# Splitting the last down weights beside the gate products, the rest from tile 1 on, and half of the first LoRA matrices asked for by GpSimd

## The chip, the cores and the metric

One core of one Trainium2 chip. The metric is the device time of one execution in microseconds (us), lower is better. TensorE (PE) multiplies, VectorE (DVE), ScalarE (ACT) and GpSimd (POOL) work on elements, SyncE (SP) mostly asks for transfers; SP, ACT and POOL each have a queue of their own for those requests (SPq, ACTq, POOLq in the rows).

## What is computed

128 sequences of 32 tokens with 512 features, so 4096 tokens; two adapted layers, of which the first contains all that the change touches:

```python
def _L0_cond_ref(x, adapter_mapping, W, b, lora_As, lora_Bs):    # A, B: one rank-16 pair per sequence
    base_out = jnp.einsum('bti,oi->bto', x, W) + b
    A, Bm = lora_As[adapter_mapping], lora_Bs[adapter_mapping]
    return base_out + jnp.einsum('btr,bro->bto', jnp.einsum('bti,bir->btr', x, A), Bm) * SCALING
def _L0_ffn_ref(x, W_gate, W_up, W_down):                        # 512 -> 1376 -> 512
    h = jax.nn.silu(x @ W_gate.T) * (x @ W_up.T)
    return h @ W_down.T
x = x + _L0_ffn_ref(_L0_cond_ref(x, slots, ...), W_gate, W_up, W_down)
x = x + _L1_ffn_ref(_L1_cond_ref(x, languages, ...), ...)        # routed low-rank experts, no nonlinearity between
```

## The kernel before, in words

Every float32 operand of a product is split in two parts that TensorE takes at full rate: ScalarE writes the high part (`..._hi`), VectorE subtracts it from the original and writes the low part (`..._lo`). A product is then three: high by high, high by low, low by high (`mm3`). The tokens are cut into `NT` = 8 tiles of 512; `KC` = 4 chunks of 128 features; `NF` = 11 chunks of the 1376 hidden features, `NP` = 5 pairs of them and one single; `NS` = 4 pairs of tiles.

**The prologue** goes over the tiles t = 0 to 7 (the first adapted linear layer). For each tile TensorE runs base products for four output chunks (`cond_base`), the tile's A products after the second chunk (`lora_in`; in tile 0 before the last quarter of the base products), and at the end the B products (`cond_lora`). ScalarE copies the four closed banks out (`close_c`, line 1015), GpSimd stores them to a scratch tensor (line 942). The A matrices of a tile come as `NG` = 2 groups of `GB` = 8 sequences, one small request (32 KB, 256 B rows) per sequence, on SyncE's queue: `gather_a`, line 559. Each takes its address from a register, which `load_slots` (line 550) fills from a table that must have landed. A group of the next tile can be asked for once `a_lo` of the same group is made for this tile. ScalarE and VectorE turn them to `a_hi`, `a_lo` (`turn_a`, lines 998 and 1437). B rows come by an indirect gather on GpSimd's queue (`gather`, line 816), whose row numbers `row_i` VectorE makes from `slot_i`.

**Weights of the feed-forward part** are also split once and stored to scratch tensors in memory. They are combined first, in a scheme with seven products in place of eight: each block needs four sums, made by GpSimd (`gate_up_sums`, `down_sums`). Gate and up weights are made beside the products of the first pair of tiles, `LEAD` = 10 products ahead, in a ring `wring` of 12 slots, and are stored from there (line 574). Down weights are made in `d_steps`: three groups (two pairs of chunks, two pairs, one pair) of seven steps, and one step for the single chunk. A step is a high part (`down_hi`, line 1042, ScalarE), a low part (`down_lo`, line 1467, VectorE) and a store on SyncE's queue (`store_down`, line 624), from four buffers `dt`. `load_down` (line 612) fetches the raw weights into two buffers `wd_raw`. `d_due(t, m)` says which step stands behind closing chunk m of tile t: one for each from (0, 1) to (5, 2), 22 steps in all. All these buffers lie in the region that the operands of the gate products take later.

**The order on each engine is fixed by the program**, and every wait holds up all that stands behind it on its engine. On SyncE a tile's turn is: requests for A of the next tile and x of the tile after (`load_x`, line 545), `load_down`, `load_slots`, then the stores of this tile's `dt` steps.

**After the prologue**, for each pair of tiles: 77 gate and up products ("slots" of 6 matmuls), then 35 down products and the single ones. From slot 77 on the weights come back through `load_slot` (line 604), whose first call waits for all `dt` stores.

## Time and profile before

| | us |
|---|---|
| three runs | 990.55, 992.14, 992.19 (median 992.14) |
| the profiled execution | 990.57 |
| its span, first to last instruction | 988.8 |
| PE busy in it | 976.7 |
| DVE, ACT, POOL busy | 589.7, 464.2, 273.1 |
| mean granted clock of TensorE | 0.997 of full |

The profile is one execution. Times in rows are us from the span's start. A row of a timeline gives start, duration, engine, line and operation, what is written from what, how many were merged (x16), and in brackets the engine's idle time before it and what ended it. Consecutive matmuls overlap in it: each is shown with 0.39 us but they start 0.227 us apart at full clock. The prologue lies in the first 152 us.

### The profile page before, as it was taken

The page shows a single profiled execution, that of the slowest core. Times are in us where ns is not written, and L with a number is a line of the kernel's source. Part 1 is how long each engine was busy: PE and PEld are TensorE (multiplying, and loading weights), DVE is VectorE, ACT ScalarE, POOL GpSimd, SP SyncE. Part 2 cuts the span into 40 slices and gives each one's busy share as a digit, 9 for nine tenths or more (in the row PEclk, how much of TensorE's full clock was granted, in tenths as well). Part 3 has the DMA queues.
Part 4 walks back from the last instruction along what each step waited for, and adds up shares of the span by engine and source line. Part 5 has one row for each costly group of instructions (what it writes and reads, how often), then busy time and mean ns, then how long its engine had stood idle before and what let it go on. Part 6 is the DMA issues. An engine that isn't in the chain of part 4 may idle for free.

```text
span 988.8 us, 14263 instructions
## 1 busy us (share of the span) xinstructions
PE 976.7 (99%) x4723; PEld 825.7 (84%) x4723; DVE 589.7 (60%) x969; ACT 464.2 (47%) x854; POOL 273.1 (28%) x276
## 2 busy tenths in 40 slices
PE   8989999999999999999999999999999999999998
PEld 6878888888888888888888888888888899898986
DVE  4555587676794433496333398243268488786862
ACT  4654657655671333472333375233357274545342
POOL 3543343564400622310431330072140470000000
PEclk9989999999999999999999999999999999999999
DMA  7898886766977876777986787887679650606132
GB/s 236 268 389 285 278 280 233 269 215 252 323 267 249 296 238 193 249 231 257 314 278 194 207 288 247 276 304 199 192 256 347 236 191 22 237 23 234 64 107 86
DMA packets 131730, 230.14 MB, mean 233 GB/s; under 512 B 30789, under 2 KB 30790, under 8 KB 131146
## 3 DMA queue, kind: packets, MB, share of 16 engines
q1 hardware_dynamic: 127720, 216.63, 66.0%
q0 software_dynamic: 3936, 12.61, 3.5%
q8 instruction: 39, 0.64, 0.3%
q14 instruction: 33, 0.27, 0.1%
q10 hardware_dynamic: 2, 0.00, 0.0%
HBM read 165.74 MB, written 63.44 MB: 232 GB/s over the span
## 4 chain that ended last, share of the span: by engine, by line
PE 89%; SPq 4%; DVE 3%; issue 1%; DMA 1%; ACT 1%; DVEq 0%; ACTq 0%
PE bank L1863 89%; SPq L559 3%; DMA a_raw<-in_a_cols 1%; PE bank L2016 1%; DVE cop_lo L1484 1%; DVE a_lo L1437 1%; DVE dt L1467 0%; SPq L545 0%; SPq L550 0%; SPq L558 0%; DVE wring L1462 0%; ACT c_out L1015 0%; SPq L624 0%; DVE b_lo L1440 0%; DVE c L1493 0%
## 5 line engine op out<-in xcount | busy, mean ns | idle before, releaser
L1863 PE MATMUL bank<-cop_hi,wring 128*128 128x512 f32 x1234 | 380.4, 389 | 0.2 <-ACT c_out L1015 0.2
L1863 PEld LDWEIGHTS bank<-cop_hi,wring 128*128 128x128 f32 x1234 | 231.6, 188 | 48.5 <-ACT c_out L1015 0.4
L1863 PE MATMUL bank<-cop_lo,wring 128*128 128x512 f32 x616 | 239.6, 389 | 0.0
L1863 PE MATMUL bank<-op_hi,wring 128*128 128x512 f32 x560 | 173.7, 389 | 0.0
L1512 DVE TENSOR_TENSOR v<-bank,p7s 128x512 f32<-128x512 f32 x44 | 30.4, 691 | 202.9 <-PE bank L1863 202.9
L1863 PEld LDWEIGHTS bank<-cop_lo,wring 128*128 128x128 f32 x616 | 115.6, 188 | 24.0
L1863 PEld LDWEIGHTS bank<-op_hi,wring 128*128 128x128 f32 x560 | 105.1, 188 | 22.0 <-DMA wring<-wd_scratch 0.2
L1863 PE MATMUL bank<-op_lo,wring 128*128 128x512 f32 x280 | 108.9, 389 | 0.0
L1114 ACT ACTIVATE s<-bank 128x512 f32<-128x512 f32 x44 | 26.3, 599 | 119.0 <-PE bank L1863 118.7
L1498 DVE TENSOR_TENSOR op_lo<-h,op_hi 128x512 fp32r<-128x512 f32 x100 | 72.6, 743 | 3.7 <-ACT op_hi L1071 3.4
L861 POOL TENSOR_TENSOR h_t<-h,h 128x512 f32<-128x512 f32 x20 | 26.5, 1326 | 163.1 <-DVE h L1534 163.1
L1071 ACT ACTIVATE op_hi<-h 128x512 fp32r<-128x512 f32 x100 | 62.6, 626 | 13.3 <-PE bank L1863 12.4
L1083 ACT ACTIVATE bank<-bank 128x512 f32<-128x512 f32 x44 | 25.6, 582 | 77.1 <-PE bank L1863 77.1
L1863 PEld LDWEIGHTS bank<-op_lo,wring 128*128 128x128 f32 x280 | 52.6, 188 | 10.8
L900 POOL TENSOR_TENSOR t_sum<-x_second,x_second 128x256 f32<-128x256 f32 x12 | 8.9, 776 | 175.8 <-DMA x_second<-x_scratch 175.8
L1863 PE MATMUL bank<-xa_hi,w_hi 128*128 128x512 f32 x128 | 51.2, 400 | 1.6 <-DVE w_lo L1429 1.1
L1863 PE MATMUL bank<-xa_lo,w_hi 128*128 128x512 f32 x128 | 50.9, 398 | 0.0
L1863 PE MATMUL bank<-xa_hi,w_lo 128*128 128x512 f32 x128 | 50.7, 396 | 0.0
L1517 DVE TENSOR_TENSOR p7s<-bank,p7s 128x512 f32<-128x512 f32 x44 | 30.4, 692 | 24.8 <-PE bank L1863 24.6
L1090 ACT ACTIVATE p7s<-bank 128x512 f32<-128x512 f32 x44 | 26.3, 599 | 30.6 <-PE bank L1863 30.6
L1105 ACT ACTIVATE s<-bank 128x512 f32<-128x512 f32 x44 | 26.3, 598 | 30.6 <-PE bank L1863 30.6
L1098 ACT ACTIVATE bank<-bank 128x512 f32<-128x512 f32 x44 | 25.6, 582 | 30.0 <-PE bank L1863 30.0
(226 smaller groups left out, 1932.6 us busy)
## 6 DMA issues: line engine op xcount, KB each, us to landing
wring<-wgu_scratch SPq DMA_DIRECT2D x231, 256.0 KB, 3.0
wring<-wd_scratch SPq DMA_DIRECT2D x140, 256.0 KB, 5.5
wgu_scratch<-wring SPq DMA_DIRECT2D x77, 256.0 KB, 3.4
c_scratch<-c_out POOLq DMA_DIRECT2D x32, 256.0 KB
c<-c_scratch SPq DMA_DIRECT2D x32, 256.0 KB, 4.1
xs_raw<-x_scratch SPq DMA_DIRECT2D x16, 512.0 KB, 5.6
out<-res SPq DMA_DIRECT2D x32, 256.0 KB, 2.1
x_raw<-in_x SPq DMA_DIRECT2D x15, 512.0 KB, 6.5
```

The lines of the kernel that those rows point to most:

```text
L559: e.dma_start(a_raw[:, g, b, :], a_cols[bass.ds(slot, 1)].rearrange("s p c -> (s p) c")).then_inc(a_in[g], DMA)
L861: e.tensor_tensor(h_t3[p][:, :], h22[p][:, :], h12[p][:, :], ALU.subtract).then_inc(t3_done, 1)
L1071: e.activation(op_hi[n % N_OP][:, :], op_source[i][p][:, :], ACT.Copy).then_inc(op_hi_done, 1)
L1083: e.activation(bank_y[b][:, :], bank_a[b][:, :], ACT.Copy).then_inc(ay_done, 1)
L1090: e.activation(p7s[b][:, :], bank_w[b][:, :], ACT.Copy).then_inc(p7s_done, 1)
L1098: e.activation(bank_z[b][:, :], bank_y[b][:, :], ACT.Copy).then_inc(yz_done, 1)
L1105: e.activation(s1[j % 2][:, :], bank_a[j % 2][:, :], ACT.Silu).then_inc(silu1_done, 1)
L1114: e.activation(s2[j % 2][:, :], bank_z[j % 2][:, :], ACT.Silu).then_inc(silu2_done, 1)
L1498: e.tensor_tensor(op_lo[n % N_OP][:, :], op_source[i][p][:, :], plain(op_hi[n % N_OP][:, :]), ALU.subtract).then_inc(op_lo_done, 1)
L1512: e.tensor_tensor(v[b][:, :], bank_z[b][:, :], p7s[b][:, :], ALU.add).then_inc(gc22_done, 1)
L1517: e.tensor_tensor(p7s[b][:, :], bank_y[b][:, :], p7s[b][:, :], ALU.add).then_inc(gc21_done, 1)
L1863: return e.matmul(out_ap, lhs, rhs, start=start, stop=stop, skip_group_check=True)
```

## The change

Three things, which do not depend on each other's values:

- GpSimd asks for the second group of tile 0's A: it waits for the table, loads 8 registers and issues 8 requests ahead of its gather of B. SyncE asks for the first group alone. The load of `slot_i` goes from SyncE's queue to ScalarE's.
- The two large groups of down steps (14) stand from chunk 1 of tile 1 to chunk 0 of tile 5: three steps in tile 1, three in tile 2, four in tile 3, three in tile 4, one in tile 5 (`d_at`). `load_down(0)` and `load_down(1)` go to the ends of SyncE's turns for tiles 0 and 1.
- The last group and the single chunk, now two halves (9 steps), go beside the gate products of the first pair, one step in each block of seven from block 1 to block 9 (`d_late`), with buffers of their own. They are loaded at the start of that stage, their sums stand behind `gate_up_sums(3)` on GpSimd, and each store stands on SyncE behind a gate store. `load_c(1, 0)`, which fills one of the borrowed regions, waits for the last step; the seventh operand of the down products waits for all stores.

```diff
--- before.py
+++ after.py
...
+    within(cst_region, 5 * ROW)
+    wd_late = work("wd_late", [2, D], F32)
+    wd_single = work("wd_single", [D], F32)
+    ds_late = [work(f"ds_late{i}", [2 * P], F32) for i in range(4)]
+    dt_late = [sb(f"dt_late{i}", [2, 2 * P], F32R, op_region + n * ROW)
+               for i, n in enumerate((N_OP - 2, N_OP - 1, 2 * N_OP - 2, 2 * N_OP - 1))]
...
     a_in = [sem(f"a_in{g}") for g in range(NG)]
-    b_in = sem("b_in")
+    a_first_in, b_in = sem("a_first_in"), sem("b_in")
     c_stored = [sem(f"c_stored{m}") for m in range(KC)]
...
     dt_stored = [sem(f"dt_stored{i}") for i in range(4)]
-    ws_stored = sem("ws_stored")
     w_moved = [sem(f"w_moved{i}") for i in range(N_W)]
...
     n_groups = (NP + 1) // 2
-    d_steps = [(g, i) for g in range(n_groups) for i in W_ORDER]
+    d_steps = [(g, i) for g in range(n_groups) for i in W_ORDER] + [("s", b) for b in range(2)]
     d_turn = {st: n for n, st in enumerate(d_steps)}
+    N_D, N_EARLY = len(d_steps), len(W_ORDER) * (n_groups - 1)
+    d_at = [KC + 1 + n * (KC * (NT - 3) - 3) // N_EARLY for n in range(N_EARLY)]
...
-        n = KC * t + m - 1
-        return [n] if 0 <= n <= len(d_steps) else []
-    def dt_stores(r):
-        return len([n for n in range(len(d_steps)) if n % 4 == r])
+        return [n for n in range(N_EARLY) if d_at[n] == KC * t + m]
+    def d_late(j):
+        return [N_EARLY + j - 1] if 0 < j <= N_D - N_EARLY else []
+    def dt_stores(r, steps=N_D):
+        return len([n for n in range(steps) if n % 4 == r])
...
     def d_views(n):
-        if n == len(d_steps):
-            src = wd_raw[n_groups % 2][:, 0, 0, :].rearrange("p (b c) -> p b c", b=2)
-            return dt_[n % 4][:, :, 0, :], dt_[n % 4][:, :, 1, :], src
         g, i = d_steps[n]
+        if g == "s":
+            return dt_late[n % 4][:, 0, :], dt_late[n % 4][:, 1, :], wd_single[:, 2 * P * i:2 * P * (i + 1)]
+        if g == n_groups - 1:
+            src = {1: wd_late[:, 0, 0:2 * P], 2: wd_late[:, 1, 0:2 * P], 4: wd_late[:, 1, 2 * P:],
+                   5: ds_late[0][:, :], 6: ds_late[1][:, :], 7: ds_late[2][:, :], 3: ds_late[3][:, :]}[i]
+            return dt_late[n % 4][:, 0, :], dt_late[n % 4][:, 1, :], src
         c, r = pairs_of(g), wd_raw[g % 2]
...
                 e.wait_ge(cop_lo_done, cop_n(s, q, C_ORDER[0]) - 1)
+            if (s, q) == (1, 0):
+                e.wait_ge(dt_lo_done, N_D)
             if s > 1 and q == 0:
...
                     e.wait_ge(dt_stored[r], DMA * dt_stores(r))
-                e.wait_ge(ws_stored, DMA)
             if n == N_SLOT:
...
         def load_down(g):
-            if g >= 2:
-                e.wait_ge(dt_lo_done, d_turn[g - 2, 3] + 1)
-            if g < n_groups:
-                n = pairs_of(g)
-                src = w_down[:, 4 * g:4 * g + 2 * n, :].rearrange("p (r k) d -> p r k d", r=n)
-                e.dma_start(wd_raw[g % 2][:, 0:n, :, :], src).then_inc(wd_in[g % 2], DMA)
-            else:
-                e.dma_start(wd_raw[g % 2][:, 0, 0, :], w_down[:, 2 * NP, :]).then_inc(wd_in[g % 2], DMA)
+            n = pairs_of(g)
+            e.dma_start(wd_raw[g][:, 0:n, :, :], w_down[:, 4 * g:4 * g + 2 * n, :].rearrange(
+                "p (r k) d -> p r k d", r=n)).then_inc(wd_in[g], DMA)
+        def load_down_late():
+            e.wait_ge(cop_lo_done, 14)
+            e.dma_start(wd_late[:, :, :], w_down[:, NF - 3:NF - 1, :]).then_inc(wd_in[0], DMA)
+            e.dma_start(wd_single[:, :], w_down[:, NF - 1, :]).then_inc(wd_in[1], DMA)
...
             e.wait_ge(dt_lo_done, n + 1)
-            if n == len(d_steps):
-                e.dma_start(ws_dram,
-                            plain(dt_[n % 4][:, :, :, :]).rearrange("p b h c -> p b (h c)")).then_inc(ws_stored, DMA)
+            g, i = d_steps[n]
+            if n >= N_EARLY:
+                to = ws_dram[:, i, :] if g == "s" else wd_dram[g, i][:, 0, :]
+                e.dma_start(to, plain(dt_late[n % 4][:, :, :]).rearrange("p h c -> p (h c)")).then_inc(
+                    dt_stored[n % 4], DMA)
                 return
-            g, i = d_steps[n]
             c = pairs_of(g)
...
             e.dma_start(w0_raw[:, part, :], w0[:, part, :]).then_inc(w0_in[ks[0]], DMA)
-        e.dma_start(slot_i[:, :], slots.unsqueeze(1).to_broadcast([GB, R, n_batch // GB])).then_inc(slots_in, DMA)
         e.wait_ge(slot_list_in, DMA)
         load_slots(0)
-        gather_a(0)
+        gather_a(0, (0,))
         for ks in x_parts(1):
             load_x(1, ks)
-        load_down(0)
         load_slots(1)
...
                     load_x(t + 2, ks)
-            if t == 1:
-                load_down(1)
+            if t < 2:
+                load_down(t)
             if t + 2 < NT:
...
                     store_down(n)
-                    for g in (2, 3):
-                        if n == d_turn[g - 2, 3]:
-                            load_down(g)
+        load_down_late()
         for n in range(7, N_G):
...
                 load_gate_up(n // 7 + 2)
+            if (n - LEAD) % 7 == 6:
+                for k in d_late((n - LEAD) // 7):
+                    store_down(k)
+        for j in range((N_G - LEAD) // 7, NF):
+            for k in d_late(j):
+                store_down(k)
         for n in range(N_G, NS * N_SLOT + N_W):
...
             e.wait_ge(wd_in[g % 2], DMA * (g // 2 + 1))
-            if g > 0:
-                e.wait_ge(dt_lo_done, d_turn[g - 1, 3] + 1)
-            s1_, s2_, s3_, s4_ = (b[:, 0:n, :] for b in ds)
-            r = wd_raw[g % 2]
-            a11, a12 = r[:, 0:n, 0, 0:2 * P], r[:, 0:n, 1, 0:2 * P]
-            a21, a22 = r[:, 0:n, 0, 2 * P:], r[:, 0:n, 1, 2 * P:]
+            if g < n_groups - 1:
+                if g > 0:
+                    e.wait_ge(dt_lo_done, d_turn[g - 1, 3] + 1)
+                s1_, s2_, s3_, s4_ = (b[:, 0:n, :] for b in ds)
+                r = wd_raw[g]
+                a11, a12 = r[:, 0:n, 0, 0:2 * P], r[:, 0:n, 1, 0:2 * P]
+                a21, a22 = r[:, 0:n, 0, 2 * P:], r[:, 0:n, 1, 2 * P:]
+            else:
+                s1_, s2_, s3_, s4_ = (b[:, :] for b in ds_late)
+                a11, a12, a21, a22 = (wd_late[:, k, half:half + 2 * P] for half in (0, 2 * P) for k in range(2))
             e.tensor_tensor(s1_, a21, a22, ALU.add).then_inc(ds_done, 1)
...
             pattern=[[-1, P]], channel_multiplier=1).then_inc(pool_const, 1)
+        slot_regs = [e.alloc_register(f"pool_slot{n}") for n in range(GB)]
+        e.wait_ge(slot_list_in, DMA)
+        e.reg_load(slot_regs, slot_sb[0:1, GB:2 * GB])
+        for b in range(GB):
+            slot = e.snap(slot_regs[b], min_val=0, max_val=a_cols.shape[0] - 1)
+            e.dma_start(a_raw[:, 1, b, :], a_cols[bass.ds(slot, 1)].rearrange("s p c -> (s p) c")).then_inc(a_first_in, DMA)
         gather(0)
...
                 for n in d_due(t, m):
-                    if n < len(d_steps) and d_steps[n][1] == W_ORDER[0]:
+                    if d_steps[n][1] == W_ORDER[0]:
                         down_sums(d_steps[n][0])
...
                     gate_up_sums(j + 2)
+                if s == 0 and j == 1:
+                    down_sums(n_groups - 1)
                 if s > 0 and j == 1:
...
             for g in range(NG):
-                e.wait_ge(a_in[g], GB * DMA * (t + 1))
+                if (t, g) == (0, 1):
+                    e.wait_ge(a_first_in, GB * DMA)
+                else:
+                    e.wait_ge(a_in[g], GB * DMA * (t + 1 - g))
                 if t > 0:
...
             hi, _, src = d_views(n)
-            if n == len(d_steps):
-                e.wait_ge(wd_in[n_groups % 2], DMA * (n_groups // 2 + 1))
+            g, i = d_steps[n]
+            if g == "s":
+                e.wait_ge(wd_in[1], 2 * DMA)
+            elif i in S_OF:
+                e.wait_ge(ds_done, 4 * g + S_OF[i])
             else:
-                g, i = d_steps[n]
-                if i in S_OF:
-                    e.wait_ge(ds_done, 4 * g + S_OF[i])
-                else:
-                    e.wait_ge(wd_in[g % 2], DMA * (g // 2 + 1))
+                e.wait_ge(wd_in[g % 2], DMA * (g // 2 + 1))
             if n >= 4:
...
                 for r in range(4):
-                    e.wait_ge(dt_stored[r], DMA * dt_stores(r))
-                e.wait_ge(ws_stored, DMA)
+                    e.wait_ge(dt_stored[r], DMA * dt_stores(r, N_EARLY))
             if s > 0 and (q, i) == (0, C_ORDER[0]):
...
                 e.wait_ge(pe_slot, slot_n(s0, "d", *op_order[r]) + 1)
+            if n == N_OP - 2:
+                for r in range(4):
+                    e.wait_ge(dt_stored[r], DMA * dt_stores(r))
             if i == 1:
...
         e.dma_start(slot_sb[0:1, :], slot_list).then_inc(slot_list_in, DMA)
+        e.dma_start(slot_i[:, :], slots.unsqueeze(1).to_broadcast([GB, R, n_batch // GB])).then_inc(slots_in, DMA)
         split_x(0)
...
                     make(s, j, k)
+                if s == 0:
+                    for n in d_late(j):
+                        down_hi(n)
                 if j % 2 == 1:
...
                 make(s, j, (3, 4, 5, 6))
+                if s == 0:
+                    for n in d_late(j):
+                        down_lo(n)
                 if j % 2 == 1:
...
             for n in range(NP, N_OP):
```

## Rows read from the trace of the kernel before

**Rows 1.** Busy time by engine, from the page.
```profile
PE 976.7 (99%) x4723; PEld 825.7 (84%) x4723; DVE 589.7 (60%) x969; ACT 464.2 (47%) x854; POOL 273.1 (28%) x276
```
**Rows 2.** TensorE's waits over the span: total us, times, longest.
```profile
PE bank L1863 <- DVE a_lo L1437: 5.1, 3, 2.5
```
**Rows 3.** Windows around the stall: busy us by engine, granted clock, DMA share, GB/s.
```profile
68.00:72.00 4.00, 1.48 (x12) 1.17 (x11) 0.84 (x2) 1.50 (x3) 0.00 (x0) 0.63 1.03 379
72.00:76.00 4.00, 4.00 (x16) 3.73 (x17) 4.00 (x7) 2.25 (x5) 2.68 (x2) 0.52 1.01 349
```
**Rows 4.** Timelines of ScalarE (tile ends) and TensorE (tile 3's A products).
```profile
24.96 1.32 ACT L1015 ACTIVATE c_out<-bank,b 128x512 f32<-128x512 f32 x2 [0.85 <-PE bank L1863]
...
41.55 0.69 ACT L1015 ACTIVATE c_out<-bank,b 128x512 f32<-128x512 f32 x1 [3.98 <-PE bank L1863]
...
58.23 0.69 ACT L1015 ACTIVATE c_out<-bank,b 128x512 f32<-128x512 f32 x1 [2.63 <-PE bank L1863]
...
67.59 0.39 PE L1863 MATMUL bank<-xa_hi,a_hi 128*128 128x256 f32 x1 [1.77 <-DVE a_lo L1437]
...
81.61 0.69 ACT L1015 ACTIVATE c_out<-bank,b 128x512 f32<-128x512 f32 x1 [4.88 <-PE bank L1863]
```
**Rows 5.** Chain of waits, 28 to 80 us: shares by line, then pieces.
```profile
by line: SPq L559 41.2%; PE bank L1863 15.9%; DVE dt L1467 8.9%; issue 8.9%; DMA a_raw<-in_a_cols 7.3%; SPq L545 5.3%; SPq L550 3.4%; SPq L624 3.4%; SPq L558 2.7%; DVE a_lo L1437 2.5%; SPq L612 1.8%; ACT a_hi L998 1.2%
...
31.48 0.61 DVE a_lo L1437
...
66.68 3.79 DMA a_raw<-in_a_cols
```
**Rows 6.** Timeline of SyncE's queue: requests for A of tiles 0, 2 and 3.
```profile
6.14 8.22 SPq L559 DMA_DIRECT2D a_raw<-in_a_cols  x16
...
32.26 13.41 SPq L559 DMA_DIRECT2D a_raw<-in_a_cols  x16
...
52.47 7.81 SPq L559 DMA_DIRECT2D a_raw<-in_a_cols  x8
...
61.59 5.42 SPq L559 DMA_DIRECT2D a_raw<-in_a_cols  x8
```
**Rows 7.** Timelines around tile 0's A and B; last, GpSimd's stores as one group.
```profile
11.76 1.35 POOL L816 DMA_INDIRECT b_raw<-in_b_rows,row_i  x1 [10.10 <-DVE row_i L1712]
...
18.04 0.63 ACT L998 ACTIVATE a_hi<-a_raw 128x512 fp32r<-128x512 f32 x1 [4.79 <-DMA a_raw<-in_a_cols]
...
18.58 1.13 ACT L1003 ACTIVATE b_hi<-b_raw 128x512 fp32r<-128x512 f32 x2
...
19.45 0.39 PE L1863 MATMUL bank<-xa_hi,a_hi 128*128 128x256 f32 x1 [0.78 <-DVE a_lo L1437]
...
L942 POOL DMA_DIRECT2D c_scratch<-c_out x32 | 17.8, 560 | 34.6 <-ACT c_out L1015 34.4
```
**Rows 8.** VectorE groups beside GpSimd's sums (24:33, 84:93) and mostly without (58:63.5).
```profile
L1467 DVE TENSOR_TENSOR dt<-wd_raw,dt 128x512 fp32r<-128x512 f32 x3 | 4.7, 1602 | 1.8 <-ACT dt L1042 1.8
...
L1437 DVE TENSOR_TENSOR a_lo<-a_raw,a_hi 128x512 fp32r<-128x512 f32 x2 | 2.4, 1223 | 0.0
...
L1467 DVE TENSOR_TENSOR dt<-ds,dt 128x512 fp32r<-128x512 f32 x1 | 0.7, 678 | 0.0
```
**Rows 9.** Timelines in the gate stage: GpSimd's sums of block 4, VectorE's `v`.
```profile
175.93 0.74 POOL L832 TENSOR_TENSOR gs<-wg_raw,wu_raw 128x256 f32<-128x256 f32 x1 [7.07 <-DMA wu_raw<-in_w_up]
...
187.56 0.69 DVE L1512 TENSOR_TENSOR v<-bank,p7s 128x512 f32<-128x512 f32 x1 [1.76 <-PE bank L1863]
```
**Rows 10.** First down weights: request, first use; then median landing of such transfers.
```profile
248.45 2.66 SPq L604 DMA_DIRECT2D wring<-wd_scratch  x5
...
256.72 0.39 PE L1863 MATMUL bank<-op_hi,wring 128*128 128x512 f32 x1
...
wring<-wd_scratch SPq DMA_DIRECT2D x140, 256.0 KB, 5.5
wgu_scratch<-wring SPq DMA_DIRECT2D x77, 256.0 KB, 3.4
```

## The prediction, made before the changed kernel was run

> **What bounds the kernel now.** I read the page's busy table first: TensorE is busy for 976.7 of 988.8 us [rows 1], so nothing but its gaps can be won without taking products away, and the change takes none away. The next view is TensorE's own waits. Their largest entry is three waits for `a_lo`, the low half of a tile's LoRA matrix A: 5.1 us in all [rows 2]. All three lie in the first eight passes over the tiles (the prologue). The timeline of TensorE and ScalarE says where and what they cost. ScalarE's first `c_out` copy of a tile marks the tile's end. From tile 1 to tile 2 these marks are 58.23 - 41.55 = 16.68 us apart, from tile 2 to tile 3 they are 81.61 - 58.23 = 23.38 us apart [rows 4]. So 6.70 us are lost in tile 3. 1.77 + 2.5 = 4.3 us of it are the two longer waits [rows 2, 4]; the other 2.4 us are the products behind them: the granted clock reads 0.63 and 0.52 of full in the eight microseconds that hold the second gap and what follows [rows 3], so it was mostly at the lower level (1.2 GHz). The third wait is 0.78 us, at 19.45 [rows 7].
>
> Then the chain of waits over 28 to 80 us, to see who makes `a_lo` late. 41% of it is line 559, the requests for A on SyncE's queue; it runs from VectorE's `a_lo` at 31.48 through one request after another to the last one at 66.68, which lands 3.79 us later [rows 5]. SyncE is never idle for long in it: tile 2's sixteen requests took 13.41 us from 32.26, tile 3's first eight 7.81 from 52.47 and its other eight 5.42 [rows 6]. And it began at 31.48 only because VectorE had three `dt` subtractions in front, 4.7 us for three [rows 8]. So the stall at tile 3 is made by a queue that started late at tile 2.
>
> **The change, part by part.** I write T for the time of a tile's first `c_out`. TensorE came to tile 3's A products at 67.59 - 1.77 = 65.82, so 7.6 us after T = 58.23 [rows 4]; the second group's follow after 12 products of 256 columns, at half of 0.227 us each (1.4 us).
>
> (a) Second half of tile 0's A asked for by GpSimd. It removes 8 of 16 requests from SyncE: half of 8.22, 4.1 us [rows 6], and 0.8 more as the small `slot_i` load goes to ScalarE's queue. `slot_i`'s issue on ScalarE falls in front of its first activation, which waits for x anyway: nothing, bounded by its 0.8 us on SyncE if it did delay x. GpSimd gets a register load and 8 requests. No row has such a request on GpSimd. Lower bound: its plain stores, 0.56 each [rows 7]; upper bound: its indirect gather, 1.35, and about 0.3 between two [rows 7], so 1.65. I take 0.75, near the plain one, whose form it has, with something for reading the register. SyncE made its first request at 6.14 behind a load of 16 registers [rows 6]; with 8 registers I let GpSimd begin at 5.4. This makes 6.0 us: requests out by 11.4. Behind them in GpSimd's order stands the gather of B, which started at 11.76 before [rows 7]: unmoved. A's second half lands by about 15 instead of being copied at 18.04 after 4.79 of idle time [rows 7]. The 0.78 wait and the slip at its restart go: **-0.9**. Next late there is B: `b_hi` ran at 18.58 straight behind `a_hi`, so B had landed by then, and the last 12 base products (2.7 us), which now start near 20, hide the B side up to about 22.7.
>
> (b) The down halves leave tile 0. `load_down(0)` goes to the end of tile 0's loop, three `dt` steps go to tile 1. VectorE is free for tile 1's `a_lo` some 4 us earlier (before it had 4.7 us of `dt` in front, [rows 8]), so SyncE starts tile 2's sixteen requests at about 27 instead of 32.26. At the old pace they end at 40.5; `load_x`, `load_down(1)`, the slots, 43.6; then `store_down` waits for VectorE's third `dt` step of tile 1, 44.7, which is new, and behind it tile 3's requests. These wait in any case for tile 2's first `a_lo`, about 46.5, against 52.47 before [rows 6]. At the old pace (61.6 + 5.4 - 52.5 = 14.5 us for sixteen and an x load) they end at 61.1 and land by 64.9. TensorE is 0.9 early, so tile 2 has T = 57.3 and the second group's low half is wanted at 66.3; a copy of 0.63 and a subtraction of 0.70 make it 66.2. So even at the old pace it just fits, and about 1 MB less is queued in front (three stores of 0.5 MB for four, and no third load). **-6.7**, with the clock kept. If the requests go slower than that, up to the 3 us of (R1).
>
> (c) Steps 6 to 9 and the sums of the second group now meet at tile 3. `down_sums(1)` may start when step 6 is done, some 2.0 us after T, and takes GpSimd about 6.3 us; in that time VectorE has three `dt` steps and then tile 4's first `a_lo`. The nearest rows: three `dt` steps beside `down_sums(0)` took 1.60 each instead of 0.68; two `a_lo` beside the short `down_sums(2)` took 1.22 each [rows 8]. At 1.6 each the first `a_lo` is done at T + 2.3 + 3 x 1.6 + 1.6 = T + 8.7; at 1.2 at T + 7.1; wanted at T + 7.6. Price 0 to 1.5 us with the restart; **+1.2** taken, as the sums are the long ones. In tile 0 it fitted: T = 24.96, `a_lo` done at 31.48 + 0.61, T + 7.1 [rows 4, 5], because the sums had started before T.
>
> The Trainium skill (SBUF — State Buffer, Who interferes with whom) says that a VectorE instruction with two SBUF inputs and a GpSimd instruction that reads SBUF lock each other out for the whole instruction. By that VectorE gets one step through for each GpSimd sum, four sums cover three `dt` and the `a_lo`, and the wait would be 1.5 instead of my 1.2; the 4.7 us for three steps [rows 8] agree.
>
> (d) Last group and the single row, nine steps, beside the gate products of the first pair. ScalarE gets 0.4 us, VectorE 0.4 to 0.7 per block of seven products (9.5 us). VectorE idled 1.76 us before its next `v` in a block with GpSimd busy, more in the others; GpSimd idled 7.07 us before the fourth block's sums, and `down_sums(2)` needs 4 x 0.75 [rows 9]. Covered: **0**. If the cover failed in each of nine blocks it would be 0.4 each, 3.6.
>
> (e) The new wait: `load_slot(77)`, the first down weights, waits until all `dt` stores have landed, and all of SyncE's loads stand behind it. The ninth step is made at 248.2 (old time), its store issued at about 248.3 behind the last gate store, landed 3.4 us later, 251.7 [rows 10], where the load was issued at 248.45. It has then to land by 256.72 [rows 10]: 5.0 us. The median over all such loads is 5.5, these first ones find an emptier queue. Price 0 to 1; 0 taken.
>
> (f) Tiles 4 to 6. Tiles 4 and 5 now have four steps of the large size instead of six of the small one and the single row; a tile's sixteen requests (8 to 14.5 us [rows 6]) and the rest of its queue fit in 16.7 us unless the DMA engines fill. **0**, and the other end is R1.
>
> Sum: -0.9 - 6.7 + 1.2 = -6.4. The profiled execution took 990.57 (span 988.8 and 1.8 around it), so 984.2. The median of the three runs is 1.6 above it; I put the forecast half way, **985.0**.
>
> **The rivals.** (R1) The stall moves: the requests are slow because the DMA engines are full (1.03 and 1.01 of their time around the stall [rows 3]), not because the queue began late. Then tile 3 or 4 still waits 1 to 2 us and pays for the clock: 2 to 4 us given back, 987 to 989. For it: that share; against it: 1 MB less in front and the earlier start. (R2) New waits in the gate or down stage, (d) or (e): 1 to 3 us, 986 to 988. (R3) The change doesn't do what it says: VectorE's `a_lo` for tile 2 is held by x or B instead, SyncE starts no earlier, the stall of tile 3 stays: 991, at most 0.9 from (a). Against it: x for tile 2 is asked for earlier too. (R4) Slower than before: a request with a register address costs GpSimd 1.65. Then the eight end at 18.6, A's second half is copied after 22.4 and wanted at 18.5, and the B gather comes 6.8 late; the two waits overlap and together make 5.3 (18.5 to 23.8) to 6.8; I take 5.7, and 2.4 for the clock as at tile 3, against 5.5 won elsewhere: 990.57 - 5.5 + 8.1 = 993.2, with the 0.8 of above 994. It decides from about 1.3 us per request.
>
> The Trainium skill (SBUF — State Buffer, SBUF: two separate sides) warns of this way: descriptors for GpSimd's DMAs are written by GpSimd and wait while VectorE holds the shared port, 0.62 us becoming 3.1. It ties that to VectorE's two-port modes, which by the same page `tensor_tensor` has not. The plain stores [rows 7], many of them issued beside `tensor_tensor`, average 0.56 and show no such thing.
>
> **How the numbers follow.** Forecast (983 to 986.5): 0.62. R1 0.14, R2 0.10, R3 0.07, R4 0.07. The range goes from 982.6 (the sum without (c), and a lower run) to 989.0, which leaves out R3 and R4. A measurement tells about 0.2%, 2 us, from no change: faster means below 990.1. Forecast, R1 and R2 are faster (0.86, less 0.02 for their ends), R3 mostly the same, R4 slower.
>
> **What would show it.** Right: TensorE's waits for `a_lo` fall from 5.1 to about 1, at tile 4; the marks of tile ends [rows 4] are 16.7 apart at tile 3; tile 2's requests start near 27; granted clock 1.00 throughout; no wait for `wring` at the change to down products. Wrong: GpSimd requests over 1.3 us; requests for tile 3 past 62; a clock below 1 anywhere behind the start.

## The result, and the profile after

| | before | after |
|---|---|---|
| median | 991.7 (990.55 to 992.19, 4 runs) | 985.57 (984.73 to 986.78, 4 runs) |
| the profiled execution | 990.57 | 985.77 |
| its span | 988.8 | 984.1 |
| tile 3, mark to mark | 23.38 | 16.68 |

All in us. The median of before is that of four runs, the three of above and one more, 991.27. The ratio after to before is 0.9941, 95% interval 0.9924 to 0.9958. The forecast was 985.0 in a range of 982.6 to 989.0. One execution of all those below, 1215.57 us at a granted clock of 0.75 (the late group alone), was in a slow state and is left out of every figure.

A tile's **mark** is the start of its first `c_out`, as in the prediction, and a tile's length is the distance from the mark before it to its own.

Busy time of the changed kernel, from the page; it answers to [rows 1]:

```profile
PE 974.5 (99%) x4723; PEld 823.9 (84%) x4723; DVE 591.9 (60%) x970; ACT 463.7 (47%) x855; POOL 277.6 (28%) x284
```

As many products, in 2.2 us less: those slowed by the clock are gone. TensorE's waits (total us, times, longest), against [rows 2]:

```profile
PE bank L1907 <- DVE r_i L1747: 1.6, 1, 1.6
PE bank L1907 <- issue: 1.5, 1, 1.5
PE bank L1907 <- ACT c_out L1051: 1.2, 2, 1.0
PE bank L1907 <- DVE w_lo L1470: 0.9, 1, 0.9
PE bank L1907 <- DMA wring<-wd_scratch: 0.5, 1, 0.5
```

The 5.1 us for `a_lo` have left the list, and a wait called "issue" is new. ScalarE's timeline, the first `c_out` of a tile, against [rows 4]:

```profile
23.89 2.76 ACT L1051 ACTIVATE c_out<-bank,b 128x512 f32<-128x512 f32 x4 [0.84 <-PE bank L1907]
```

The marks of tiles 0 to 7, all read like this one, are 23.89, 40.47, 57.15, 73.83, 92.29, 108.97, 128.04 and 145.24; before they were 24.96, 41.55, 58.23, 81.61, 98.29, 114.97, 133.49 and 150.68. The lead is therefore 1.08 us up to tile 2, 7.78 after tile 3, 6.00 after tile 4, 5.45 after tile 6. One later mark of each kernel, before and after, in the first pair's down products:

```profile
311.31 0.58 ACT L1083 ACTIVATE bank<-bank 128x512 f32<-128x512 f32 x1 [16.65 <-PE bank L1863]
```
```profile
305.90 0.58 ACT L1120 ACTIVATE bank<-bank 128x512 f32<-128x512 f32 x1 [16.34 <-PE bank L1907]
```

The lead is still 5.41 us: nine down steps more in this stretch cost nothing. At the end it is 988.8 - 984.1 = 4.7.

SyncE's queue after, the requests for A of tiles 1, 2 and 3, against [rows 6]:

```profile
16.10 8.68 SPq L575 DMA_DIRECT2D a_raw<-in_a_cols  x16
...
29.07 9.00 SPq L575 DMA_DIRECT2D a_raw<-in_a_cols  x16
...
47.90 6.09 SPq L575 DMA_DIRECT2D a_raw<-in_a_cols  x8
...
54.65 3.99 SPq L575 DMA_DIRECT2D a_raw<-in_a_cols  x8
```

Tile 2's sixteen start 3.2 us earlier and take 4.4 us less, so that tile 3's end at 58.64 instead of 67.01. Tile 4's own A is where the new wait is; VectorE and TensorE there:

```profile
76.17 5.01 DVE L1508 TENSOR_TENSOR dt<-wd_raw,dt 128x512 fp32r<-128x512 f32 x3 [0.41 <-ACT dt L1077]
81.10 2.35 DVE L1478 TENSOR_TENSOR a_lo<-a_raw,a_hi 128x512 fp32r<-128x512 f32 x2
```
```profile
82.96 0.36 PE L1907 MATMUL bank<-xa_hi,a_hi 128*128 128x256 f32 x1 [1.53 <-issue]
```

Three `dt` steps and two `a_lo` take 7.3 us, while GpSimd makes the four sums of `down_sums(1)` (75.92 to 82.31). The first of the two `a_lo` takes 1.75 us and ends at 82.85. The wait bears the name "issue", but the product at 82.96 takes this `a_lo`. Windows around it (busy us by engine, granted clock, DMA share, GB/s) show the clock whole, unlike [rows 3]:

```profile
80.00:84.00 4.00, 2.46 (x16) 1.92 (x15) 4.00 (x5) 2.48 (x5) 4.00 (x6) 1.00 0.84 298
```

### The profile page after: what moved, and what is told of

It is laid out like the page before. It is cut to its first block, busy times and chain, and to the rows that moved or that the text cites. A ratio compares the mean times of both kernels' runs of the same rounds, so it can differ in the third digit from the quotient of the medians.

```text
span 984.1 us, 14271 instructions
## 1 busy us (share of the span) xinstructions
PE 974.5 (99%) x4723; PEld 823.9 (84%) x4723; DVE 591.9 (60%) x970; ACT 463.7 (47%) x855; POOL 277.6 (28%) x284
## 4 chain that ended last, share of the span: by engine, by line
PE 92%; DVE 3%; DMA 2%; issue 1%; ACT 1%; POOL 0%; SPq 0%; ACTq 0%; DVEq 0%
PE bank L1907 92%; DMA wring<-wd_scratch 1%; PE bank L2060 1%; DMA x_raw<-in_x 1%; DMA b_raw<-in_b_rows,row_i 1%; DVE cop_lo L1525 0%; DVE a_lo L1478 0%; DVE b_lo L1481 0%; DVE wring L1503 0%; ACT c_out L1051 0%; DVE h_masked L1491 0%; ACT lh_hi L1045 0%; DVE c L1534 0%; DVE c L1530 0%; DVE xa_lo L1466 0%
```

## The experiments

Each is compared with the kernel before on its own chip (medians 991.3 to 991.7).

### The parts alone

**(a) alone: the requests on GpSimd and `slot_i` on ScalarE's queue, put into the kernel before.**

```diff
-        gather_a(0)
+        gather_a(0, (0,))
...
+            e.dma_start(a_raw[:, 1, b, :], a_cols[bass.ds(slot, 1)]...).then_inc(a_first_in, DMA)
         gather(0)
```

> The kernel before with the GpSimd part alone (A's second half of tile 0 asked for by GpSimd, slot_i on ScalarE's queue). Theory Q (the stall of tile 3 is SyncE's queue starting late behind VectorE's dt steps of tile 0): the end of tile 0 comes 1.1 us earlier, as in the changed kernel (24.96 to 23.89), the marks of tile ends from tile 2 to 3 stay 22 to 23.4 us apart, and the span falls by 0.8 to 1.5 us. Rival G (it was SyncE's eight requests less that freed the queue): tile 3 takes 16.7 us and the span falls by 5 to 6 us.

(Beside this, the single chunk's store counts on one of the `dt` semaphores and no longer on its own, as in the changed kernel.)

Measured: 990.78, ratio 0.9998 (0.9988 to 1.0009): nothing. Neither expectation came true: tile 0 ends at 27.10, 2.1 us later than before and not 1.1 earlier, and tile 3 is 18.11 us long, not 22 to 23.4. ScalarE says why tile 0 is late:

```profile
14.51 1.15 ACT L1005 ACTIVATE a_hi<-a_raw 128x512 fp32r<-128x512 f32 x2 [0.95 <-DMA a_raw<-in_a_cols]
19.95 1.16 ACT L1010 ACTIVATE b_hi<-b_raw 128x512 fp32r<-128x512 f32 x2 [4.29 <-DMA b_raw<-in_b_rows,row_i]
```

A comes early, but SyncE, relieved of eight requests, asks for x and the raw down weights 4.6 us sooner, which here is ahead of the gather of B. `b_hi` ran at 17.57 in the changed kernel, which has x there but not the raw weights, and runs at 19.95 here. VectorE's work behind it moves by 2.4 us as well, then `lh_lo` meets the first GpSimd sum and takes 1.53 us instead of 0.69, and TensorE waits 4.0 us for it. Against the kernel before, this edit loses 2.1 us in tile 0, 1.5 in tile 1 (granted clock 0.71 in its first microseconds), 1.4 in tile 6 and 0.5 in tile 7, and wins 5.3 in tile 3. The win is not one of earlier requests: tile 3's end at 66.50 instead of 67.01. TensorE itself is 3.6 us late at tile 2's mark, so it waits less for them.

**The shift alone: all 22 steps packed from chunk 1 of tile 1 on, none in the gate stage.**

```diff
-        n = KC * t + m - 1
-        return [n] if 0 <= n <= len(d_steps) else []
+        return [n for n in range(len(d_steps) + 1) if KC + 1 + n * 19 // 22 == KC * t + m]
...
-        load_down(0)
...
-            if t == 1:
-                load_down(1)
+            if t < 2:
+                load_down(t)
```

> The kernel before with the shift alone: all 22 dt steps from chunk 1 of tile 1 to chunk 3 of tile 5, loads at the ends of the turns; SyncE asks for all of tile 0's A and nothing goes to the gate stage, so the prologue moves as many bytes as before. Theory Q: TensorE's wait for a_lo at 19.45 (0.78) stays, tile 3 takes 16.7 us, one collision of GpSimd's sums with VectorE of up to 1.8 us comes in, and the span falls by 4 to 6 us. Rival B (the stall is full DMA engines, and only fewer bytes in the prologue cure it): tile 3 or a later tile still waits 2 us or more with the granted clock falling, and the span falls by 3 us at most.

Measured: 992.93, ratio 1.0018 (1.0008 to 1.0029). The expectation (tile 3 at 16.7 us, 4 to 6 us won) was wrong. The rival's figures came (tile 3 waits 3.2 us in one piece, granted clock 0.80 and 0.77 behind it), but not for its reason: with as many bytes in the prologue as before, tile 3's requests end at 61.67 instead of 67.01. Tile 3 is still 21.62 us long for another cause. ScalarE in front of it:

```profile
65.46 0.63 ACT L1040 ACTIVATE dt<-wd_raw 128x512 fp32r<-128x512 f32 x1 [2.70 <-DMA wd_scratch<-dt]
66.00 1.13 ACT L996 ACTIVATE a_hi<-a_raw 128x512 fp32r<-128x512 f32 x2
```

There are four `dt` buffers, so a step waits until the store of the step four before it has landed. That store stands on SyncE behind requests for A, and `a_hi` stands behind the step. The last stores, now close to the gate stage, cost another wait (3.4 us at `c_out` in tile 6). So this packing of 22 steps costs more than it wins; with 14 the same shift works.

**The changed kernel without (a).**

```diff
-        gather_a(0, (0,))
+        gather_a(0)
...
-            e.dma_start(a_raw[:, 1, b, :], a_cols[bass.ds(slot, 1)]...).then_inc(a_first_in, DMA)
```

(and the load of `slot_i` back on SyncE's queue)

> The changed kernel without its GpSimd part. Theory Q: tile 0 ends 1.1 us later than in the changed kernel, with the wait of 0.8 for a_lo back; tile 3 stays at 16.7 us, tile 4 at 18.5; the span is 1.1 us over the changed kernel's, 3.6 to 4.3 under that of before. Rival G: tile 3's stall comes back, in part at least, and the span is 3 us or more over the changed kernel's.

Measured: 986.42, ratio 0.9956 (0.994 to 0.9973), as expected. Tile 3 is 16.68 us long; tile 0 ends at 24.99 instead of 23.89. So in the changed kernel (a) is worth 1.1 us at tile 0 and has no part in tile 3.

**The late group alone: nine steps beside the gate products, the other 14 and both loads as before.**

```diff
-    d_at = [KC + 1 + n * (KC * (NT - 3) - 3) // N_EARLY for n in range(N_EARLY)]
+    d_at = [1 + n for n in range(N_EARLY)]
```

(an edit of the kernel without (a), with `load_down` back at its old places.)

> Only the third of the change's parts: the last group and the single chunk go beside the gate products of the first pair; the other 14 steps stand as in the kernel before, one behind each chunk from chunk 1 of tile 0, with both loads where they were; no requests by GpSimd. Theory (the stall of tile 3 is made in tile 0, by VectorE's lock and by the bytes that are queued ahead of tile 2's requests, none of which this edit touches): tile 3 keeps its stall, its mark 22 to 23.5 us behind tile 2's, and the gate stage costs nothing; median 990 to 992. Rival: it is the amount of steps per tile that counts, and with the last group gone the queue drains: tile 3 below 19 us, 986 to 988. Second rival: the late steps cost something that the shift hides: the first pair's gate stage is longer than 159.9 us, 992 and more.

Measured: median 986.72 of nine runs, ratio 0.9959 (0.9946 to 0.9973). The expectation was wrong and the figures of its rival came true: this part alone, which leaves the steps of tile 0 as they were, brings two thirds of the gain by the ratios. Its requests for A, tiles 2 and 3:

```profile
33.28 10.33 SPq L575 DMA_DIRECT2D a_raw<-in_a_cols  x16
...
50.84 7.63 SPq L575 DMA_DIRECT2D a_raw<-in_a_cols  x8
...
59.53 4.37 SPq L575 DMA_DIRECT2D a_raw<-in_a_cols  x8
```

They end at 63.90, 3.1 us before the old 67.01, tile 2's mark is 1.0 us later than before (59.20), and tile 3 is 18.16 us long, 5.2 less. Not all of this can be put down to the edit: up to 44 us nothing in the order of the requests is changed, and yet tile 2's sixteen took 10.33 us here and 13.41 and 13.52 in two profiles of before. Why is open. Tile 6 is 17.28 us long instead of 18.52: the gate weights are asked for 3.8 us sooner (110.04 against 113.84 in the changed kernel), and the first gate sums are done at 122.4, before the first `cop_lo` at 124.6, where in the changed kernel both run from 122.8 on and `cop_lo` takes 1.23 us instead of 0.69. The nine runs form two groups, five from 985.5 to 986.7 and four from 988.3 to 988.6; the traced one is the fastest of the first, so what is read here need not hold for the second.

### What makes the requests late

**Tile 0's sums one tile later, in the kernel before.**

```diff
+                if (t, m) == (1, 1):
+                    down_sums(0)
                 for n in d_due(t, m):
-                    if n < len(d_steps) and d_steps[n][1] == W_ORDER[0]:
+                    if 0 < n < len(d_steps) and d_steps[n][1] == W_ORDER[0]:
```

> The kernel before, with GpSimd's sums down_sums(0) moved from chunk 1 of tile 0 to chunk 1 of tile 1; nothing else is moved. The first group's dt steps stay where they are, so those that read a sum come later. Question: is the lock of VectorE by these sums (dt 1.60 us each instead of 0.68) what made tile 2's requests for A late? Theory: it is only a part. The steps of tile 0 that need no sum drop to about 0.7 us, VectorE is free up to 2.7 us earlier, but SyncE still carries load_down(0), the dt stores and x in front; tile 2's sixteen requests start at 29.5 to 31 instead of 32.26, at the old pace of about 13 us, and half or less of tile 3's stall goes: tile 3's mark 20 to 22.5 us behind tile 2's (23.38 before), median 988.5 to 991. Rival: the lock is the whole cause: requests start before 29.5, tile 3 is 16.7 us long, about 985. Other rival: a step that waits for its sum holds back A behind it and the time is worse, 992 or more.

Measured: 989.24, ratio 0.9974 (0.996 to 0.9988). The three `dt` steps took 0.69 us each. The requests started only at 32.07, since SyncE still had x and the three stores in front, but took 9.70 us instead of 13.41, with the same stores in front, and tile 3 was 16.68 us long. The median lies in the range of the theory, but by luck: start, pace and tile 3 were all outside it. The sums then locked tile 2's operands:

```profile
34.06 7.27 DVE L1427 TENSOR_TENSOR xa_lo<-x_raw,xa_hi 128x512 fp32r<-128x512 f32 x4 [1.86 <-ACT xa_hi L989]
```
```profile
43.38 0.39 PE L1865 MATMUL bank<-lh_hi,b_hi 128*128 128x256 f32 x1 [2.95 <-DVE lh_lo L1458]
```

Four `xa_lo` of 0.6 us took 7.27, TensorE waited, its granted clock was 0.58 in the four microseconds from 44 on, and tile 1 was 19.82 us long, tile 2 18.20. A stall was cured and another one made, and the second did most of the curing: tile 3's requests ended 2.0 us earlier than before, and TensorE reached tile 2's mark 4.4 us later.

**Tile 0's `dt` stores behind tile 2's requests, in the kernel before.**

```diff
+                for n in range(3):
+                    store_down(n)
...
-                    store_down(n)
+                    if t > 0:
+                        store_down(n)
```

(the first two lines stand behind tile 2's requests.)

> The kernel before, with one edit: the three dt stores of tile 0 (0.5 MB each) stand on SyncE behind tile 2's sixteen requests for A instead of in front of them. Question: what makes the requests slow, 13.41 us for sixteen before and 9.00 in the changed kernel? Theory (what lies queued in front): the requests start at 31 to 32, since VectorE's a_lo is still behind three dt subtractions, but take 9 to 10.5 us, end at 41 to 42.5, and tile 3's wait for a_lo falls below 1 us: tile 3 at most 18 us long, median 986 to 988.5. Rival (the pace is SyncE's own or the whole load of the DMA engines in those microseconds): 13 us again, ends at 44.5 to 45.5, the stall of tile 3 stays at 5 to 6.7 us, 990 to 992.

Measured: 994.25, ratio 1.0029 (1.0018 to 1.004). About the pace the theory was right (8.54 us, even below its 9 to 10.5), about the time it was wrong:

```profile
31.70 8.54 SPq L559 DMA_DIRECT2D a_raw<-in_a_cols  x16
```
```profile
49.66 0.63 ACT L1045 ACTIVATE dt<-ds 128x512 fp32r<-128x512 f32 x1 [6.88 <-DMA wd_scratch<-dt]
```

Without the 1.5 MB of stores in front, the sixteen take 8.54 us. But the fifth `dt` step waits for the first buffer's store, 6.88 us, the same trap as in the shift alone; tile 2 was 24.95 us long, tile 3 16.67. That tile 3 has no stall here shows nothing for the early requests: its requests end at 68.66, later than before, but tile 2's mark is 7.7 us later too.

**The kernel before once more.**

> The kernel before once more, unedited, for a second profile. Question: do tile 2's sixteen requests for A take 13.41 us each time, or is that pace a matter of the execution? In e9_late_alone, where everything up to 44 us is in the same order as here, they took 10.33 us. Theory: the pace varies from one execution to the next, since with the same order in front it was 13.41 before, 11.01 in e1_gpsimd_alone and 10.33 in e9_late_alone; so 10 to 14 us here, and the run's time moves with it: below 991 with a pace near 10 to 11 and a stall of tile 3 of 3 to 6 us, 991 to 992 with one near 13. Rival: it is fixed by the program: 13.2 to 13.6 again, marks within 0.1 us of the first profile, tile 3 23.3 to 23.5 us long; then something in e9_late_alone's layout made the difference.

Measured: 991.47, ratio 0.9995 (0.9983 to 1.0007); the profiled execution took 992.05. The sixteen requests took 13.52 us from 33.22: the rival on the pace was right. The marks were not the same, though. Tile 1 is 17.31 us long instead of 16.59 and tile 7 18.64 instead of 17.19. Tile 3 is 22.17 us long instead of 23.38: its two waits make 3.7 us instead of 4.3, and the granted clock read 0.60 and 0.97 in the windows 68:72 and 72:76, where the first profile has 0.63 and 0.52 [rows 3]. Single requests in the chain of waits, in the first profile of before (the first, third and fifth of the sixteen, the sixth, and the last):

```profile
32.26 0.80 SPq L559
...
34.17 1.04 SPq L559
...
36.71 1.65 SPq L559
...
38.55 0.33 SPq L559
...
43.87 1.80 SPq L559
```

A request takes SyncE 0.33 us, and they start 0.52 us apart. Five took 0.7 to 1.7 here, at a DMA share of 1.03 and 1.05, and one 1.80 late, without a visible reason. In the late group alone, with the same order in front, only three were slow (0.90 to 1.11) and none late. A full share by itself does not make them slow: in the changed kernel it is as high (0.98, 1.00 and 1.20 in the windows from 28 to 40 us), and its sixteen took 9.00 us. The windows, before and after:

```profile
32.00:36.00 4.00, 4.00 (x31) 3.77 (x30) 4.00 (x8) 2.08 (x4) 3.24 (x5) 1.00 1.03 417
```
```profile
32.00:36.00 4.00, 4.00 (x28) 3.67 (x28) 3.19 (x5) 1.96 (x5) 0.00 (x0) 1.00 1.00 415
```

What stands in front has a part in it, but not alone: the sixteen took 8.4 to 10.2 us in the nine profiles without tile 0's stores in front and 9.7 to 13.5 in the five with them.

All profiles in one table; "lag" is the end of tile 3's requests minus the mark of tile 2, so a small lag is good. It falls when the requests come earlier, and also when TensorE itself is late; the two columns in front of it tell which. All in us:

| kernel | tile 2's requests: start, length | tile 3's end at | mark of tile 2 | lag | tile 3 long |
|---|---|---|---|---|---|
| before | 32.26, 13.41 | 67.01 | 58.23 | 8.8 | 23.38 |
| before once more | 33.22, 13.52 | 67.80 | 59.13 | 8.7 | 22.17 |
| (a) alone | 33.38, 11.01 | 66.50 | 61.85 | 4.65 | 18.11 |
| late group alone | 33.28, 10.33 | 63.90 | 59.20 | 4.70 | 18.16 |
| shift alone | 29.39, 10.17 | 61.67 | 58.27 | 3.4 | 21.62 |
| stores behind | 31.70, 8.54 | 68.66 | 65.94 | 2.7 | 16.67 |
| after without (a) | 30.78, 9.11 | 60.74 | 58.27 | 2.5 | 16.68 |
| sums later | 32.07, 9.70 | 64.96 | 62.60 | 2.4 | 16.68 |
| after | 29.07, 9.00 | 58.64 | 57.15 | 1.5 | 16.68 |
| five more with all three parts | 28.95 to 30.42, 8.4 to 9.6 | 58.80 to 59.43 | 57.15 to 58.16 | 1.3 to 1.8 | 16.68 |

Tile 3's length goes with the lag: at 2.7 us the stall is gone, at 4.7 it is 1.5 us, and the next 4 us of lag cost 4 to 5.2 more, since the clock falls as well. The shift alone stands outside: there `dt` held `a_hi`. In the late group alone and in the kernels with the shift it is mostly the requests that come earlier; in (a) alone, stores behind and sums later most of the smaller lag is TensorE's own delay, and these kernels gain little or nothing.

### The lock at tile 4

**`down_sums(1)` at chunk 1 of tile 4, in the changed kernel.**

```diff
-                for n in d_due(t, m):
-                    if d_steps[n][1] == W_ORDER[0]:
-                        down_sums(d_steps[n][0])
+                for g, at in ((0, (1, 1)), (1, (4, 1))):
+                    if (t, m) == at:
+                        down_sums(g)
```

> The changed kernel with down_sums(1) one tile later on GpSimd (behind the gather of tile 5's B, from 84 us on). Theory L (TensorE's 1.53 us at tile 4 is VectorE held by GpSimd's sums): the three dt steps of tile 3 take 0.69 each again, the wait at 82.96 goes, the marks from tile 3 to 4 are 16.7 apart instead of 18.46, and the span is 1.8 us below the changed kernel's. Rival: the lock only moves to the next tile's x_lo or lh_lo and TensorE waits 0.5 to 1.5 us there; or tile 4's wait was the requests for A, then it stays.

Measured: 984.14, ratio 0.9933 (0.9917 to 0.995). VectorE behind tile 3:

```profile
78.41 0.69 DVE L1508 TENSOR_TENSOR dt<-wd_raw,dt 128x512 fp32r<-128x512 f32 x1 [0.41 <-ACT dt L1077]
79.01 1.29 DVE L1478 TENSOR_TENSOR a_lo<-a_raw,a_hi 128x512 fp32r<-128x512 f32 x2
```

As expected: each step is back at 0.69 us, tile 4 is 16.68 us long, the "issue" wait is gone. Nothing else was moved, so the sums beside VectorE's steps are the cause of tile 4's wait. One `lh_lo` is locked later (1.64 us), which TensorE does not feel.

**This kernel and the changed one again, on one chip.**

> e4_sums_later once more (GpSimd's down_sums(1) from chunk 0 of tile 3's neighbourhood to chunk 1 of tile 4), side by side with the changed kernel. It was 984.14 against 985.57. Expected: 1.4 to 2 us faster than the changed kernel on the same chip, from tile 4 alone (16.68 us against 18.46). If the difference is below 0.7 us, the cure of the lock is real but given back later in the run.

> The changed kernel once more, on the same chip as the next one. It was 985.57 us. Question: do the 0.5 us recur that TensorE waited at 742 us for a down weight of the last pair, which the kernel before did not show? If they come from where the transfers happen to fall, they will be another amount or absent, with everything up to 311 us within 0.1 us of the first profile; if they belong to the change, 0.4 to 0.6 again.

Measured: 983.96 (ratio 0.9923, 0.9903 to 0.9943) against 985.59 (0.9937, 0.9916 to 0.9957): 1.63 us apart, as expected. The changed kernel's tile 4 is 18.44 us long again; its tile 6 is 18.52, so the 19.07 of the first profile belonged to that execution. At 743 us TensorE waits 0.73 us for a down weight, neither the same as before nor absent. It was 0.3 to 1.2 us in five profiles, all of kernels with (a), and missing in two others with (a) and in all without. Its cause is open.

**In addition, the first gate sums of tile 6 held until the seventh `cop_lo`.**

```diff
+                if m == 2 and t == NT - 2:
+                    e.wait_ge(cop_lo_done, 7)
```

> The changed kernel with GpSimd's down_sums(1) at chunk 1 of tile 4 (as in e4_sums_later) and, in addition, the first gate sums behind the chunk 2 of tile 6 held until VectorE has made its seventh cop_lo. Theory: the 0.5 us that the changed kernel loses in tile 6 (19.07 against 18.52) is a GpSimd sum that locks one more cop_lo, so tile 6 comes back to 18.5 or less, and the run is 0.4 to 1.0 us faster than e4_sums_later: 983.2 to 983.9 median. Rival: the sums then lock a_lo of tile 7, or the first gate weights come late: TensorE waits for wring at the first slots, 984.5 and more.

Measured: 984.99, ratio 0.9931 (0.9919 to 0.9943). The rival was right. Tile 6 comes to 17.28 us, but the sums then run beside VectorE's work for tile 7, and that tile takes 19.59 us instead of 17.2 (an `a_lo` or `b_lo` alone takes 0.69, two 1.29):

```profile
127.42 2.00 DVE L1480 TENSOR_TENSOR a_lo<-a_raw,a_hi 128x512 fp32r<-128x512 f32 x2 [0.52 <-ACT a_hi L1036]
129.35 2.37 DVE L1483 TENSOR_TENSOR b_lo<-b_raw,b_hi 128x512 fp32r<-128x512 f32 x2
```

### The price of a request on GpSimd

**Each of the eight requests twice, in the changed kernel.**

```diff
+            e.dma_start(wd_raw[1][:, 0, 0, b * KC * R:(b + 1) * KC * R],
+                        a_cols[bass.ds(slot, 1)]...).then_inc(a_first_in, DMA)
             e.dma_start(a_raw[:, 1, b, :], a_cols[bass.ds(slot, 1)]...).then_inc(a_first_in, DMA)
```

> The changed kernel, where GpSimd issues ahead of each of its eight requests for A a second one of the same size and form, from the same place in memory into a buffer that nobody reads at that time: sixteen requests in front of the gather of B. This prices a request with a register address, on which the slower rival rests. Expected from 0.58 us per request in the changed kernel's trace: sixteen take 9.3 us, the gather of B comes at about 13.1 instead of 10.57, b_hi some 2.5 us later (20 instead of 17.57), A's second half later by up to 4.7 us at its last request; TensorE waits 1 to 2.5 us more in tile 0, its mark at 25 to 26.5 instead of 23.89, and the loss stays to the end: 986.5 to 988.5. By the slower rival's reckoning (decides from about 1.3 us per request; here 1.16 per useful request) the two waits are still small. Rival: the queue of GpSimd takes the second eight more slowly (1 us and more each), the gather comes behind 16, 989 and more.

Measured: 986.28, ratio 0.9949 (0.9933 to 0.9965), 0.7 us over the changed kernel and a little less than expected. GpSimd in the changed kernel, then one of the sixteen and the gather here:

```profile
3.76 4.67 POOL L938 DMA_DIRECT2D a_raw<-in_a_cols  x8 [1.99 <-issue]
10.57 1.03 POOL L836 DMA_INDIRECT b_raw<-in_b_rows,row_i  x1 [2.14 <-DVE row_i L1753]
```
```profile
8.72 0.54 POOL L940 DMA_DIRECT2D a_raw<-in_a_cols  x1
...
12.87 1.36 POOL L836 DMA_INDIRECT b_raw<-in_b_rows,row_i  x1 [0.30 <-issue]
```

The sixteen take from 3.76 to 12.57, 0.55 us each, and TensorE waits 0.86 us for `a_lo` at tile 0 (mark 24.88). Even a doubled price eats only the gain of (a).

## Why the prediction was right, step by step

**The sum.** It was -0.9 - 6.7 + 1.2 = -6.4 against the profiled execution. The marks gave -1.08 (tile 0), -6.70 (tile 3), +1.78 (tile 4), +0.55 (tile 6) and 0.7 lost late: -4.8 in that pair of profiles, so the sum promised 1.6 us too much for the execution that it was worked out from: (c) was 0.6 short, and tile 6 and the late loss were in no term. The medians are 6.1 apart, and between 985.57 and the forecast of 985.0 lie 0.6 us. That it came so close is in part luck: the profiled execution of before was 1.1 us faster than its median, which no term explains, and the 0.8 that the forecast added for it made up for half of what the sum lacked. Against the second profile of before (992.05) the difference is 6.3 us, but made of other pieces (tiles 1 and 7 are longer there, tile 3 is shorter).

**(a), right.** -0.9 was taken, -1.08 measured. Taken at 0.75 us, a request costs 0.58, or 0.55 on the average of sixteen; the plain stores [rows 7] were the nearest row, and the slower rival (R4), which needed 1.3, is out. GpSimd began at 3.76, not 5.4. What the step left out: SyncE moves up as well. In the changed kernel no raw down weights are in that gap, so nothing collides; alone, in the old program, the same edit brings nothing.

**(b), right in its size, partly wrong in its path.** VectorE made `a_lo` of tile 1 at 27.20, against 31.40: the 4 us of the prediction. But the requests began at 29.07, not 27. SyncE was itself busy: tile 1's requests until 24.77, x and the load until 27.20, then registers for a table of slots, a step of `load_slots` that took 1.78 us in the chain of before:

```profile
47.29 1.78 SPq L550
```

The prediction counted these before tile 3's requests and forgot them before tile 2's. A second error made it good, by luck: "at the old pace" was 13.4 us, measured 9.00. Moving the three stores away is enough for such a pace (8.54), but 9.70 was also measured with them in front, so how much of the 4.4 us is theirs is open. The stall did not move (R1): the DMA share of the changed kernel is still 0.84 to 1.04 there, in windows of 4 us from 44 to 68 us, but the requests were early enough. The step also read the cause too narrowly. It put the cure on tile 0 being cleared, but the late group alone leaves tile 0 as it was and has 18.16 us at tile 3: 4 us less lag were enough for most of it, wherever they came from. In the ratios the shift adds next to nothing beyond that (0.9956 against 0.9959, intervals overlapping); in the traced runs, what it wins at tile 3 it pays with (c) and at tile 6, where the late group alone has 17.28.

**(c), right, its term too small.** +1.2 was taken, +1.78 measured: 1.53 of wait and 0.25 behind it, with no loss of clock. The steps beside the sums took 5.01 / 3 = 1.67 us, against 1.60 in the rows that the price was taken from [rows 8]. By the rule of the Trainium skill (SBUF — State Buffer, Who interferes with whom), by which a VectorE instruction with two SBUF inputs and a GpSimd instruction that reads SBUF lock each other out for their whole length, the prediction worked out a wait of 1.5 us. The trace agrees: the three `dt` steps and the first `a_lo` take 1.6 to 1.8 us each beside four sums, one to a sum, and the wait is 1.53, though the inputs of the working were rounder than that. The experiment that parts the two engines gets the 1.6 us back.

**(d) and (e), right.** The lead is 5.44 us at tile 7's mark and 5.41 at the mark in the down products, and no wait for `wring` stands at the change to them. The wait of (e) did come, on SyncE: the last late store was issued at 242.84 and the first down weights asked for at 245.64, which is 251.1 in the old time (the prediction had 251.7, before it was 248.45). TensorE did not feel it. **(f)** holds in the second profile of the changed kernel (tile 6: 18.52, as before) and misses by 0.55 in the first. **R2** came only as the 0.3 to 1.2 us at 743 us, a place that the prediction did not name. **R3** is out.

## What to carry to other kernels

A stall at a queue's end is cured by asking earlier, and it does not matter where the time comes from: measure how far the last request of a tile lies behind a mark of the tile, find from which distance the stall is gone, and take the cheapest edit that gets there. Look at both ends of that distance, since it also shrinks when the reader is late, and then nothing is won. Large stores queued in front of many small requests can slow them, but here the same order took 9.7 us once and 13.5 another time, so one trace is not enough to price it. Every GpSimd sum has to run beside VectorE work that nobody waits for: moving it from one tile to the next is free only where that tile's VectorE has time to spare (tile 4, 1.6 us won; tiles 1 and 7, 2 to 3 us lost). The best version found is the changed kernel with `down_sums(1)` at chunk 1 of tile 4, about 984.0.

## What was not expected of the hardware

- A request with an address from a register took GpSimd 0.55 us, as much as a plain store. On SyncE one takes 0.33 us and they start 0.52 us apart. With the DMA share at 1.03 to 1.05 SyncE's rose to 0.7 to 1.7 us for three to five of sixteen. One of 1.80 us fell at 43.87, when the share was 0.77 (43.4 to 45.7); its cause is open.
- TensorE waited 1.53 us at 81.4 to 83.0 us with the granted clock at 1.00 afterwards, while two waits of 1.8 and 2.5 us, close behind one another, came with 0.63 and 0.52 [rows 3]. A single wait of 2.95 us (sums later) was followed by 0.58, one of 3.19 (shift alone) by 0.80 and 0.77.
- The same program had tile 3 at 23.38 and at 22.17 us in two executions, and the late group alone had its runs in two groups 2 us apart; that a few requests are slow in some executions would fit, but the second group has no trace.
